# Two graph layers on one core: the output bias of the second stage as one product over stacked parts

## Chip, cores and metric

The kernel runs on one core of one Trainium2 chip. The metric is the device time of one execution in microseconds (us). The core has the engines TensorE (PE, with its weight loads PEld), VectorE (DVE), ScalarE (ACT), GpSimd (POOL) and SyncE (SP), and 16 DMA engines.

## What is computed

The reference works on 6250 nodes with 256 features and 100000 edges sorted by target. Four blocks follow one another, each added to its input after a layer norm: a graph layer, a soft mixture of 8 experts, a second graph layer, and a mixture that picks one of 32 experts. The change lies in the first mixture:

```python
w = softmax(feat @ Wr + br)                      # 8 gates per node
h = relu(bn(einsum('bfd,edh->bfeh', x, W1) + b1))
h = relu(bn(einsum('bfeh,ehk->bfek', h, W2) + b2))
y = einsum('bfeh,ehd->bfed', h, Wo) + bo         # bo: 8 x 256
out = einsum('bfed,fe->bfd', y, w)
```

So every node's row gets, beside the gated outputs of the experts, the sum over the 8 experts of gate times output bias: a product of the nodes' gates (nodes x 8) with `bo` (8 x 256). This document calls it the bias product.

## The kernel before, in words

The program is one `build` with three large parts between barriers: a preparation (layer norm, first projections, and a sort of the edges into lists), the second stage (the block that begins at line 1127: graph layer one, the 8-expert mixture, and the projection for graph layer two), and the third stage (from line 1806). There are 49 tiles of 128 nodes. The second stage takes them in 13 groups: the first has one tile, the other twelve have four (`WIDTHS`, line 48). Here "wide group" means one of the twelve.

The order is written out by hand in slots: every engine runs `for s in range(SLOTS)` and does in slot s what tables fixed at build time say. The tables are `READY` (line 1232, when a group's edges are summed), `FFN` (line 1233, when its experts begin), `AT` (line 1241, the steps of an expert), `DONE`, `NORM4`, `BASE`, and `USES` (line 1250), the list of the uses of PSUM bank 3. A wide group takes 16 slots, two for each expert.

In each of the first 196 slots (`EGROUPS`) 512 edges are handled. POOL gathers their source rows with four indirect DMAs into a ring of three buffers `got` (line 1324), and before it fills a buffer again it waits for the last reader (`s_mlo`, line 1322). ACT weighs the rows (`weigh`, line 1379) and rounds them to an upper part `mhi` (`upper_messages`, line 1388). DVE makes the one-hot matrix `hot` from `iota_f` (`one_hot`, line 1593) and the lower part `mlo` (`lower_messages`, line 1601). PE multiplies `hot` with both parts (`edges`, line 1483); it waits there for `s_mlo`.

The expert steps are products of float32r operands split into an upper and a lower part, three matmuls for one product (`three`, line 1312). `layer(0, n)` and `layer(1, n)` (line 1499) and `outputs(n)` (line 1520) are PE's. Between them ACT applies `relus` (line 1395: two activations at line 1409 and a rounding copy to `hhi` at line 1414), then DVE makes `hlo` (`lower_half`, line 1606), for which the next layer waits. `rl` is one buffer for both layers, so the next `relus` waits for `lower_half` of the one before it. DVE's `add_out` (line 1617) adds the gated outputs to the node rows.

Bank 3 is shared in turn by six kinds of use (`USES`): "turn" (transposes of the normalised rows), "logit", "gateT" (transposes of the gates), "bias", "turn4" and "prod". PE fills it in slot s (`make_bank`, line 1533) at the end of its slot, after it has waited on `s_free` for every earlier use to be read. ACT (`read_bank`, line 1416) or DVE reads it in slot s + 1. Each use adds one to `s_free`. For a group, "gateT" stands in slot READY + 7 and the bias products of its two pairs of tiles in READY + 8 and READY + 9. Before the change ACT copies the transposed gates to `gateT`, a float32 tile of 8 partitions (line 1427), PE multiplies 128 columns of it at a time with `bos` (8 x 256 float32, lines 1559 to 1561), and DVE's `output_bias` (line 1669) adds the result to the rows.

What one engine does within a slot stands in a fixed order. DVE's part, around the place that the change touches (lines 1692 to 1706):

```python
if s in AT[4]: add_out(AT[4][s], s)
if s - 1 in USE_AT and USES[USE_AT[s - 1]][1] == "bias": output_bias(...)
if s + 1 < EGROUPS: one_hot(s + 1)
if s in AT[2]: lower_half(1, AT[2][s])
if ... == "prod": lower_product(USE_AT[s - 1])
if s + 1 < EGROUPS: lower_messages(s + 1)
if s in AT[0]: lower_half(0, AT[0][s])
```

PE's slot is layer(0), edges, outputs, layer(1), make_bank. ACT's is relus(1), read_bank, weigh, relus(0), the rounding of the normalised rows, square roots, upper_messages, and in the first eight slots the rounding of the expert weights, three pieces a slot, whose lower parts DVE makes (line 1798). In the last group, whose edges are long done, the slots fall otherwise: "gateT" is read in a slot in which relus(1) and lower_half(1) stand too.

At line 1345 and behind it SP loads the small arrays, `bo` among them, and `s_small` counts them to 240; DVE waits for that count in slot 1 (line 1775).

## Time and profile before

| what | us |
| --- | --- |
| three runs | 3012.72, 3002.51, 3017.39 (median 3012.72) |
| profiled execution | 3008.19 |
| its span, first to last instruction | 3006.3 |
| PE busy over the span | 2719.2 (90%) |
| DVE busy | 2165.6 (72%) |
| POOL busy | 1939.8 (65%) |
| ACT busy | 1514.5 (50%) |

Shares are of the span. The profiled execution has 1.9 us outside its span. All times of single instructions below are of that one execution, counted from the start of its span. The second stage's gathers begin at about 413 us in it, its last bias product stands at 1745 us, and the third stage's first edge product at 1856.6 us.

### The profile page before, as it was taken

The page shows a single profiled execution, that of the slowest core. Times are in us where ns is not written, and L with a number is a line of the kernel's source. Part 1 is how long each engine was busy: PE and PEld are TensorE (multiplying, and loading weights), DVE is VectorE, ACT ScalarE, POOL GpSimd, SP SyncE. Part 2 cuts the span into 40 slices and gives each one's busy share as a digit, 9 for nine tenths or more (in the row PEclk, how much of TensorE's full clock was granted, in tenths as well). Part 3 has the DMA queues.
Part 4 walks back from the last instruction along what each step waited for, and adds up shares of the span by engine and source line. Part 5 has one row for each costly group of instructions (what it writes and reads, how often), then busy time and mean ns, then how long its engine had stood idle before and what let it go on. Part 6 is the DMA issues. An engine that isn't in the chain of part 4 may idle for free. (4 is left out here: it accounts for less than half of the span.)

```text
span 3006.3 us, 53462 instructions
## 1 busy us (share of the span) xinstructions
PE 2719.2 (90%) x18949; PEld 2484.4 (83%) x18949; DVE 2165.6 (72%) x5008; ACT 1514.5 (50%) x3146; POOL 1939.8 (65%) x1692
## 2 busy tenths in 40 slices
PE   5799935899999999999999993689999999999999
PEld 5789825788888888888888873689999999999998
DVE  8898836577777877877787655767777777777762
ACT  4377636788888888888888651111111111111111
POOL 0355557777777777777777204777777777777750
PEclk9999956899999999999999996789999999999999
DMA  2133454333333233333323105888888888788860
GB/s 73 6 80 77 91 141 143 92 97 94 96 108 110 79 111 111 97 94 109 107 81 108 46 22 159 210 209 201 215 215 207 208 206 211 195 204 208 203 153 15
DMA packets 241570, 390.22 MB, mean 130 GB/s; under 512 B 43258, under 2 KB 114834, under 8 KB 241042
## 3 DMA queue, kind: packets, MB, share of 16 engines
q0 software_dynamic: 163072, 310.24, 40.6%
q1 hardware_dynamic: 77940, 74.90, 7.9%
q8 instruction: 153, 2.51, 0.3%
q10 hardware_dynamic: 288, 1.61, 0.1%
q14 instruction: 117, 0.96, 0.1%
HBM read 343.43 MB, written 43.19 MB: 129 GB/s over the span
## 5 line engine op out<-in xcount | busy, mean ns | idle before, releaser
L1324 POOL DMA_INDIRECT f_got<-h_tab,list_cols x784 | 974.9, 1244 | 287.8 <-issue 220.2
L1994 POOL DMA_INDIRECT n_got<-h_tab,edge_cols x784 | 798.9, 1019 | 263.2 <-issue 232.3
L2046 ACT ACTIVATE n_hrh<-bank 128x512 fp32r<-128x512 f32 (+1 forms) x208 | 119.3, 574 | 924.5 <-PE bank L2116 924.5
L1609 DVE TENSOR_TENSOR f_hlo<-edge_cols,f_hhi 128x1024 fp32r<-128x1024 f32 (+1 forms) x208 | 241.8, 1162 | 300.0 <-ACT f_hhi L1414 299.4
L2095 PE MATMUL bank<-n_got,n_hot_h 128*128 128x256 f32 x1168 | 352.0, 301 | 70.1 <-DMA n_got<-h_tab,edge_cols 36.2
L1384 ACT ACTIVATE f_got<-f_got,list_cols 128x256 f32<-128x256 f32 x784 | 333.9, 497 | 150.2 <-DMA f_got<-h_tab,list_cols 150.1
L1495 PE MATMUL bank<-f_mhi,f_hot 128*128 128x256 f32 x1168 | 316.2, 304 | 80.8 <-DVE f_mlo L1603 80.8
L1409 ACT ACTIVATE edge_cols<-bank,f_shf,f_scl 128x512 f32<-128x512 f32 (+1 forms) x416 | 295.2, 744 | 118.5 <-PE bank L1315 84.8
L2096 PE MATMUL bank<-n_got,n_hot_h 128*128 128x256 f32 x1168 | 338.6, 290 | 0.0
L2097 PE MATMUL bank<-n_got,n_hot_l 128*128 128x256 f32 x1168 | 338.5, 290 | 0.0
L2197 DVE TENSOR_SCALAR n_hot_h<-list_cols,rel_f,edge_cols 128x256 fp32r<-128x256 f32 (+1 forms) x784 | 252.4, 389 | 117.2 <-PE bank L2097 117.1
L1495 PEld LDWEIGHTS bank<-f_mhi,f_hot 128*128 128x128 f32 x1168 | 236.4, 202 | 96.5 <-issue 91.9
L1496 PE MATMUL bank<-f_mlo,f_hot 128*128 128x256 f32 x1168 | 305.3, 295 | 0.0
L380 POOL DMA_INDIRECT list<-runs,off_i x98 | 156.0, 1592 | 224.7 <-DVE off_i L739 101.2
L2095 PEld LDWEIGHTS bank<-n_got,n_hot_h 128*128 128x128 f32 x1168 | 231.5, 198 | 82.5 <-DMA n_got<-h_tab,edge_cols 37.9
L2224 DVE SCALAR_TENSOR_TENSOR n_hrl<-bank,n_hrh 128x512 fp32r<-128x512 f32 (+1 forms) x208 | 135.9, 654 | 160.3 <-ACT n_hrh L2046 160.3
L1603 DVE TENSOR_TENSOR f_mlo<-f_got,f_mhi 128x1024 fp32r<-128x1024 f32 x196 | 238.9, 1219 | 17.1 <-ACT f_mhi L1393 17.1
L2197 DVE TENSOR_SCALAR n_hot_l<-list_cols,rel_f,edge_cols 128x256 fp32r<-128x256 f32 (+1 forms) x784 | 248.8, 396 | 0.0
L1496 PEld LDWEIGHTS bank<-f_mlo,f_hot 128*128 128x128 f32 x1168 | 237.0, 203 | 4.1
L2096 PEld LDWEIGHTS bank<-n_got,n_hot_h 128*128 128x128 f32 x1168 | 232.3, 199 | 1.7
L2097 PEld LDWEIGHTS bank<-n_got,n_hot_l 128*128 128x128 f32 x1168 | 232.0, 199 | 0.0
L1313 PE MATMUL bank<-f_whi,f_hhi 128*128 128x256 f32 x784 | 223.2, 285 | 5.6 <-DVE f_hlo L1609 5.6
(327 smaller groups left out, 7396.3 us busy)
## 6 DMA issues: line engine op xcount, KB each, us to landing
f_got<-h_tab,list_cols POOLq DMA_INDIRECT x784
n_got<-h_tab,edge_cols POOLq DMA_INDIRECT x784, 3.8
h_tab<-acc SPq DMA_DIRECT2D x37, 128.0 KB
edge_cols<-in_w SPq DMA_DIRECT2D x16, 256.0 KB, 3.2
xn<-acc_tab SPq DMA_DIRECT2D x8, 512.0 KB, 5.8
n_rows<-acc_tab SPq DMA_DIRECT2D x8, 512.0 KB, 5.6
out_rows<-n_rows SPq DMA_DIRECT2D x8, 512.0 KB, 4.6
acc<-in_x SPq DMA_DIRECT2D x4, 896.0 KB, 8.4
```

The source lines that it names most:

```text
L1324: nc.gpsimd.indirect_dma_start(got[:, s % RING0, u, :], None, h_tab[0], bass.IndirectOffsetOnAxis(gidx0[:, s * U + u:s * U + u + 1], 0), b ...
L1384: last = nc.scalar.activation(got[:, s % RING0, u, :], got[:, s % RING0, u, :], ACT.Copy, scale=w0_f[:, c:c + 1])
L1409: nc.scalar.activation(rl[:, m, 0:w], bank[(i + m) % 3][:, 0:w], ACT.Relu, bias=shf[:, l, e, m:m + 1], scale=scl[:, l, e, m:m + 1]).then_i ...
L1495: nc.tensor.matmul(tile_bank(t), lhs, mhi[:, s % 2, u, :], start=begins, stop=False)
L1496: last = nc.tensor.matmul(tile_bank(t), lhs, mlo[:, s % 2, u, :], start=False, stop=ends)
L1603: nc.vector.tensor_tensor(mlo[:, s % 2, :, :], got[:, s % RING0, :, :], mhi[:, s % 2, :, :].bitcast(F32), ALU.subtract).then_inc(s_mlo, 1)
L1609: nc.vector.tensor_tensor(hlo[l][:, :, 0:w], rl[:, :, 0:w], hhi[l][:, :, 0:w].bitcast(F32), ALU.subtract).then_inc(s_lo[l], 1)
L1994: nc.gpsimd.indirect_dma_start(got[:, s % RING, u, :], None, h_tab[1], bass.IndirectOffsetOnAxis(gidx[:, s * U + u:s * U + u + 1], 0), bou ...
L2095: nc.tensor.matmul(tile_bank(t), w_h, m_h, start=begins, stop=False)
L2096: nc.tensor.matmul(tile_bank(t), w_h, m_l, start=False, stop=False)
L2097: last = nc.tensor.matmul(tile_bank(t), w_l, m_h, start=False, stop=ends)
L2197: last = nc.vector.tensor_scalar(table[:, s % 2, u, 0:n], iota_f[:, 0:n], rel_n[:, c:c + 1], weight[:, c:c + 1], ALU.is_equal, ALU.mult)
```

## The change

It replaces the float32 bias product by one float32r product over more rows. `gateT` and `bos` become float32r tiles of 72 partitions (`STACK`). In `gateT`, partitions 0 to 7 and 64 to 71 hold the upper part of the gates, and partitions 32 to 39 the lower part. In `bos`, partitions 0 to 7 and 32 to 39 hold the upper part of the bias and 64 to 71 its lower part. All other partitions hold zeros. One matmul then sums upper times upper, lower times upper and upper times lower.

For each group ACT makes two copies of the transposed gates in place of one, counted by `s_ghi`, and DVE subtracts the upper part from bank 3 (`lower_gates`), which now frees the bank. `lower_gates` stands in DVE's slot behind `output_bias` and ahead of `one_hot`. Once, in slot 1, DVE writes zeros (three instructions) and ACT copies the bias twice; in slot 3 DVE makes the lower part. `iota_f` moves into the place of the old `bos` (row 6 of `xn`, now with all its partitions), and `bo` is loaded into a part of `xraw`.

```diff
@@ -1180,10 +1180,13 @@
             bnt = sb3("bnt", [P, 2, EXPERTS0, F])
             gws = sb3("gws", [P, F, EXPERTS0])
             gbs = sb3("gbs", [P, EXPERTS0])
-            bos = xn[0:EXPERTS0, 6, :]
+            HI_A, LO_A, HI_B, STACK = 0, 32, 64, 64 + EXPERTS0
+            bos = sb3("bos", [STACK, D], F32R)
+            s_bos = sem("f_bos")
+            s_ghi = sem("f_ghi")
             lws = sb3("lws", [P, F, D])
             lbs = sb3("lbs", [P, D])
-            iota_f = sb3("iota_f", [P, 2 * P])
+            iota_f = xn[:, 6, :]
             got = sb3("got", [P, RING0, U, D])
             mhi = sb3("mhi", [P, 2, U, D], F32R)
             mlo = sb3("mlo", [P, 2, U, D], F32R)
@@ -1197,13 +1200,14 @@
 
             xraw, rl = (edge_cols[:, b * F * W4:(b + 1) * F * W4].rearrange("p (f n) -> p f n", f=F) for b in range(2))
             iota_i = xraw[:, 0, 0:2 * P].bitcast(I32)
+            braw = xraw[0:EXPERTS0, 1, 0:D]
             xhi = sb3("xhi", [P, F, W4], F32R)
             xlo = sb3("xlo", [P, F, W4], F32R)
             x4 = sb3("x4", [P, F, 2 * P])
             glog = sb3("glog", [P, GS, EXPERTS0])
             gate = sb3("gate", [P, 2, GS, EXPERTS0])
             gm = sb3("gm", [P, GS])
-            gateT = sb3("gateT", [EXPERTS0, W4])
+            gateT = sb3("gateT", [STACK, W4], F32R)
             hhi = [sb3(f"hhi{l}", [P, F, W4], F32R) for l in range(2)]
             hlo = [sb3(f"hlo{l}", [P, F, W4], F32R) for l in range(2)]
 
@@ -1346,7 +1350,7 @@
                         sp.dma_start(bnp[:, l, a], arr).then_inc(s_small, 16)
                 sp.dma_start(gws[:, :, :], gw.rearrange("(f p) e -> p f e", p=P)).then_inc(s_small, 16)
                 sp.dma_start(gbs[:, :], gbr.partition_broadcast(P)).then_inc(s_small, 16)
-                sp.dma_start(bos[:, :], bo).then_inc(s_small, 16)
+                sp.dma_start(braw, bo).then_inc(s_small, 16)
                 sp.dma_start(lws[:, :, :], lw.rearrange("(f p) d -> p f d", p=P)).then_inc(s_small, 16)
                 sp.dma_start(lbs[:, :], lb.partition_broadcast(P)).then_inc(s_small, 16)
                 load(0)
@@ -1420,11 +1424,15 @@
                         act.wait_ge(s_made, i + 1)
                         if g:
                             act.wait_ge(s_xlo, g)
+                        else:
+                            act.wait_ge(s_bos, 6)
                         nc.scalar.activation(pair_of(xraw, j, w), turned(w), ACT.Copy).then_inc(s_free, 1)
                     elif what == "gateT":
                         act.wait_ge(s_made, i + 1)
                         n = width(g) * P
-                        nc.scalar.activation(gateT[:, 0:n], bank[3][0:EXPERTS0, 0:n], ACT.Copy).then_inc(s_free, 1)
+                        for at in (HI_A, HI_B):
+                            nc.scalar.activation(gateT[at:at + EXPERTS0, 0:n], bank[3][0:EXPERTS0, 0:n],
+                                                 ACT.Copy).then_inc(s_ghi, 1)
                     elif what == "turn4":
                         act.wait_ge(s_made, i + 1)
                         act.wait_ge(s_wlo, NPIECE)
@@ -1471,6 +1479,10 @@
                     if s + AHEAD < EGROUPS:
                         upper_messages(s + AHEAD)
                     if s == 1:
+                        act.wait_ge(s_small, 240)
+                        act.wait_ge(s_bos, 3)
+                        for at in (HI_A, LO_A):
+                            nc.scalar.activation(bos[at:at + EXPERTS0, :], braw, ACT.Copy).then_inc(s_bos, 1)
                         act.wait_ge(s_bn, 1)
                         nc.scalar.activation(scl[:, :, :, :], bnt[:, :, :, :], ACT.Sqrt).then_inc(s_bnroot, 1)
                     for i in range(s * PACE, min(s * PACE + PACE, NPIECE)):
@@ -1555,6 +1567,8 @@
                             last = nc.tensor.transpose(bank[3][0:EXPERTS0, k * P:(k + 1) * P], gate[:, g % 2, k, :],
                                                        ident[:, :])
                     elif what == "bias":
+                        if g == 0:
+                            pe.wait_ge(s_bos, 6)
                         for k in range(w):
                             last = nc.tensor.matmul(bank[3][:, k * D:(k + 1) * D],
                                                     gateT[:, (2 * j + k) * P:(2 * j + k + 1) * P], bos[:, :],
@@ -1677,6 +1691,15 @@
                     nc.vector.tensor_tensor(rows2, bank[3][:, 0:w * D].rearrange("p (k d) -> p k d", d=D), rows2,
                                             ALU.add).then_inc(s_free, 1)
 
+                def lower_gates(i):
+
+                    _, _, g, _ = USES[i]
+                    n = width(g) * P
+                    dve.wait_ge(s_ghi, 2 * g + 2)
+                    nc.vector.tensor_tensor(gateT[LO_A:LO_A + EXPERTS0, 0:n], bank[3][0:EXPERTS0, 0:n],
+                                            gateT[HI_A:HI_A + EXPERTS0, 0:n].bitcast(F32),
+                                            ALU.subtract).then_inc(s_free, 1)
+
                 def lower_product(i):
 
                     _, _, g, j = USES[i]
@@ -1694,6 +1717,8 @@
                         add_out(AT[4][s], s)
                     if s - 1 in USE_AT and USES[USE_AT[s - 1]][1] == "bias":
                         output_bias(USE_AT[s - 1], s)
+                    if s - 1 in USE_AT and USES[USE_AT[s - 1]][1] == "gateT":
+                        lower_gates(USE_AT[s - 1])
                     if s + 1 < EGROUPS:
                         one_hot(s + 1)
                     if s in AT[2]:
@@ -1774,7 +1799,12 @@
                     if s == 1:
                         dve.wait_ge(s_small, 240)
                         nc.vector.tensor_scalar(bnt[:, :, :, :], bnp[:, :, 4], BN_EPS, None, ALU.add).then_inc(s_bn, 1)
+                        for blank in (bos[:, :], gateT[:, 0:D], gateT[:, D:2 * D]):
+                            nc.vector.tensor_scalar(blank, iota_f[0:STACK, :], 0.0, None, ALU.mult).then_inc(s_bos, 1)
                     if s == 3:
+                        dve.wait_ge(s_bos, 5)
+                        nc.vector.tensor_tensor(bos[HI_B:HI_B + EXPERTS0, :], braw,
+                                                bos[HI_A:HI_A + EXPERTS0, :].bitcast(F32), ALU.subtract).then_inc(s_bos, 1)
                         dve.wait_ge(s_bnroot, 1)
                         nc.vector.reciprocal(scl[:, :, :, :], scl[:, :, :, :]).then_inc(s_bn, 1)
                         dve.wait_ge(s_bn, 2)
```

## Rows read from the trace of the kernel before

**Rows 1.** The profile's page, first part: busy us (share of span) and instructions.

```profile
PE 2719.2 (90%) x18949; PEld 2484.4 (83%) x18949; DVE 2165.6 (72%) x5008; ACT 1514.5 (50%) x3146; POOL 1939.8 (65%) x1692
```

**Rows 2.** Stretches: length, then busy of PE, PEld, DVE, ACT, POOL; PE clock, DMA share, GB/s.

```profile
600.00:700.00 100.00, 96.76 (x610) 86.15 (x610) 76.06 (x126) 87.27 (x139) 76.73 (x65) 1.00 0.32 95
...
1500.00:1600.00 100.00, 97.41 (x620) 87.33 (x620) 78.92 (x135) 85.87 (x136) 76.17 (x62) 1.00 0.34 102
```

**Rows 3.** What PE waited for, 600 to 1600 us: total us, times, longest.

```profile
PE bank L1495 <- DVE f_mlo L1603: 24.4, 30, 2.0
PE bank L1313 <- DVE f_hlo L1609: 8.2, 6, 2.1
```

**Rows 4.** The bias product's line: PE durations in ns (min/median/max), first and last start.

```profile
L1559 PE MATMUL bank<-xn,f_gateT x98: 374/374/478, 512.5 to 1744.9; 8*128 8x256 f32 x98
```

**Rows 5.** Timeline of PE at both bias products of one group: start, us, then idle before.

```profile
1025.01 1.13 PE L1559 MATMUL bank<-xn,f_gateT 8*128 8x256 f32 x4
1026.06 0.50 PE L1313 MATMUL bank<-f_xhi,f_whi 128*128 128x512 f32 x1
...
1030.02 1.13 PE L1559 MATMUL bank<-xn,f_gateT 8*128 8x256 f32 x4
1031.33 0.36 PE L1495 MATMUL bank<-f_mhi,f_hot 128*128 128x256 f32 x1 [0.19 <-DVE f_mlo L1603]
1031.53 0.28 PE L1496 MATMUL bank<-f_mlo,f_hot 128*128 128x256 f32 x1
1031.65 0.28 PE L1495 MATMUL bank<-f_mhi,f_hot 128*128 128x256 f32 x1
```

**Rows 6.** Timeline of DVE over the same place.

```profile
1019.32 1.23 DVE L1609 TENSOR_TENSOR f_hlo<-edge_cols,f_hhi 128x1024 fp32r<-128x1024 f32 x1 [1.66 <-ACT f_hhi L1414]
...
1022.38 0.68 DVE L1597 TENSOR_TENSOR f_hot<-f_iota_f,rel_f 128x512 fp32r<-128x512 f32 x1
...
1027.09 0.69 DVE L1677 TENSOR_TENSOR xn<-bank,xn 128x512 f32<-128x512 f32 x1
1027.70 1.22 DVE L1597 TENSOR_TENSOR f_hot<-f_iota_f,rel_f 128x1024 fp32r<-128x1024 f32 x1
...
1029.96 1.22 DVE L1603 TENSOR_TENSOR f_mlo<-f_got,f_mhi 128x1024 fp32r<-128x1024 f32 x1
...
1038.15 1.21 DVE L1603 TENSOR_TENSOR f_mlo<-f_got,f_mhi 128x1024 fp32r<-128x1024 f32 x1
```

**Rows 7.** Timeline of ACT over the same place.

```profile
1020.14 0.57 ACT L1427 ACTIVATE f_gateT<-bank 8x512 f32<-8x512 f32 x1
1021.76 1.71 ACT L1384 ACTIVATE f_got<-f_got,list_cols 128x256 f32<-128x256 f32 x4 [1.05 <-DMA f_got<-h_tab,list_cols]
...
1027.30 1.06 ACT L1414 ACTIVATE f_hhi<-edge_cols 128x1024 fp32r<-128x1024 f32 x1
```

**Rows 8.** Timeline of POOL behind it: the gathers.

```profile
1030.10 1.97 POOL L1324 DMA_INDIRECT f_got<-h_tab,list_cols  x1 [0.30 <-issue]
...
1040.21 1.01 POOL L1324 DMA_INDIRECT f_got<-h_tab,list_cols  x1 [2.81 <-DVE f_mlo L1603]
```

**Rows 9.** Timeline of PE: first edge product behind the second bias product, two more groups.

```profile
614.18 0.37 PE L1495 MATMUL bank<-f_mhi,f_hot 128*128 128x256 f32 x1
...
1659.20 0.36 PE L1495 MATMUL bank<-f_mhi,f_hot 128*128 128x256 f32 x1 [0.20 <-DVE f_mlo L1603]
```

**Rows 10.** Timelines of ACT, DVE and PE in the last group.

```profile
1735.90 0.57 ACT L1427 ACTIVATE f_gateT<-bank 8x512 f32<-8x512 f32 x1
1736.03 1.23 DVE L1609 TENSOR_TENSOR f_hlo<-edge_cols,f_hhi 128x1024 fp32r<-128x1024 f32 x1 [2.43 <-ACT f_hhi L1414]
...
1739.86 1.23 DVE L1609 TENSOR_TENSOR f_hlo<-edge_cols,f_hhi 128x1024 fp32r<-128x1024 f32 x1 [2.61 <-ACT f_hhi L1414]
...
1741.29 0.40 PE L1313 MATMUL bank<-f_hhi,f_whi 128*128 128x512 f32 x1
```

**Rows 11.** Timeline of DVE in slot 1, at the stage's start.

```profile
441.87 1.29 DVE L1798 TENSOR_TENSOR f_wlo<-edge_cols,f_whi 128x512 fp32r<-128x512 f32 x2 [2.92 <-ACT f_whi L1479]
```

## Prediction, made before the changed kernel was run

> **What bounds the kernel now.** I looked first at how busy the engines are, over the whole span and then by stretches of the second stage, because the change touches only that stage. The page has PE at 90% and DVE at 72% of the span [rows 1]. From 600 to 1600 us, where the wide groups run with edges beside them, the stretches have PE at 97 of 100 us, at a granted clock of 1.00 (the upper level, 2.4 GHz), ACT at 85 to 87, DVE at 76 to 79 and POOL at 76 [rows 2]. The reader is to see in this a stage that looks bound by PE, so that time taken off PE should come straight off the total.
>
> The waits say where that holds and where it does not. Over those 1000 us PE waited 24.4 us in 30 places for the lower messages of DVE before an edge product, and 8.2 us in 6 places for a lower half of DVE [rows 3]: nearly ten groups, so three to four short waits a group. PE is late for nobody at those places; it catches up with DVE. So the question is whether one of the three waits stands right behind the bias products. I read the timelines of PE, DVE, ACT and POOL around them, in the group whose first bias product starts at 1025.01.
>
> It does. PE finishes the second bias product and then waits 0.19 us for `mlo` before the edge product at 1031.33 [rows 5]. That `mlo` is the last link of a chain on DVE: it begins with a lower half at 1019.32 that waited 1.66 us for ACT, and ends at 1029.96 + 1.22 = 1031.18. Between them stand 13 more rows of the timeline without one wait before them [rows 6]. The same wait of 0.19 to 0.67 us for `mlo` stands behind the second bias product in ten of the eleven wide groups that still have edges (the last of them at 1659.20); in the first, at 614.18, there is none, and DVE is done only 0.1 us earlier [rows 9]. So PE and DVE arrive there together. A microsecond less on PE is a microsecond more of waiting; a microsecond more on DVE is a microsecond later.
>
> **The change, part by part.** *The product itself.* The 49 float32 products have 98 PE records [rows 4], two each. Two products occupy PE from 1025.01 to 1026.06, 1.05 us; single-pass products of 256 columns follow one another at 0.12 us (1031.53 to 1031.65) [rows 5], so two take 0.24. That frees 0.81 us for two tiles, 1.6 us for a wide group, 49 x 0.405 = 20 us in all. That the new operand has 72 rows in place of 8 I cost at nothing: the edge products at that pace have 128. The Trainium skill, "FP8 and Floating Point Precision", section "TensorE Precision Notes", has true float32 as four passes through the array; four passes at the pace of the row would be 0.48 us a tile, and the trace's 0.52 agrees. What of these 20 us shortens the stage? In the eleven groups with edges PE would reach the edge product of 1031.33 some 1.6 us earlier and wait for the same `mlo`. The first product's saving lets layer 0 of the next expert start earlier, but its `relus` waits for DVE's lower half at 1028.83, which is in the chain. I take nothing, and keep 20 us as the bound on the gain.
>
> *The new subtraction on DVE.* `lower_gates` stands ahead of `one_hot` in that very chain, before the row at 1022.38. Its nearest row is `output_bias`, also 512 elements a partition with one operand in PSUM: 0.69 us long, and 1027.70 - 1027.09 = 0.61 until the next one starts [rows 6]. I take 0.61; eight partitions in place of 128 I don't count as a gain, since ACT's copy of only 8 partitions takes 0.57 us too [rows 7]. The bounds are 0.3 (half the row, if few partitions help after all) and 0.69. It lies wholly on the path: 11 x 0.61 = 6.7 us. Whoever waits behind it waits too: `one_hot`, `mlo`, the lower half that frees `relus` of the next expert, and the `mlo` at 1038.15, for which POOL's gather at 1040.21 waits 2.81 us [rows 8]. So POOL is moved with the chain; no engine passes this place on another path.
>
> *The second copy on ACT.* It adds 0.57 us for each of the 12 wide groups. In the group read ACT's next work waited 1.05 us for a gather [rows 7], which covers it; other groups have no such wait. Where it isn't covered, the rounding to `hhi` at 1027.30 ends 0.57 later than 1028.36, at 1028.93. DVE's lower half, which needs it, starts at 1028.83 now and 0.61 later after the change, so DVE's own delay covers ACT's. And does `lower_gates` wait for the copy? It would end at 1020.14 + 2 x 0.57 = 1021.3, and DVE gets there at 1022.38: no, with 1.1 us to spare. If that cover went, each group would pay up to 0.57.
>
> *The last wide group.* There lower_half(1) stands in the same slot. The gates' copy starts at 1735.90 and the lower half at 1736.03 [rows 10]. With `lower_gates` ahead of it, that half waits for both copies and the subtraction: 1735.90 + 1.14 + 0.05 + 0.61 = 1737.7, later by 1.7. The next `relus`, its lower half (1739.86 to 1741.09) and PE's layer at 1741.29 follow it link by link, with nothing between them, so I take 1.6 us. PE's saving of 1.6 us lies beside that chain. Bounds: 0 (if the saving on PE replaces it) and 1.7.
>
> *The start.* Three blanks on DVE and two bias copies on ACT in slot 1, one small subtraction in slot 3. DVE idles 2.92 us behind the blanks [rows 11], but for ACT, which now waits for the blanks (which have no row; 0.3 us each for 256 elements, an estimate from half of the 512-element row) and makes two copies of 256 elements at 0.3. ACT waits for gathers before most of its weighings there, and DVE's chain isn't reached before POOL's: I take 0, bounds 0 to 1.5. The first group has one tile and runs beside the same gathers: 0. The load of `bo` goes to another address, in its old place in SP's queue; `iota_f` is read as before: 0.
>
> **The sum** is 6.7 + 1.6 = 8.3 us slower. Against the profiled execution it makes 3008.2 + 8.3 = 3016.5. The median of the runs is 4.5 us above the profiled one and the runs spread over 15 us, so for a median I take 3012.7 + 8.3 = 3021.0. About 0.5% (15 us) is what a measurement of this kernel can tell from no change, so this forecast counts as no change, on the slow side.
>
> **Rivals.** *PE is the bound and the gain arrives.* For it: PE is at 97%. Against it: ten waits for `mlo` exactly there. It needs DVE's chain to be elastic, for instance if its start, a wait for ACT at 1019.32, moved up with PE. Full: 3012.7 - 20 = 2993; half, if the other waits of a group (1 to 2 us each) take the rest: 3003.
>
> *DVE's chain and ACT's copy add up.* Place: the read of "gateT" in DVE's slot. It decides once ACT's second copy ends later than DVE's arrival, or if POOL's late gathers no longer cover it. Price: 11 x (0.61 + 0.57) + 1.7 = 14.7, with 1.5 at the start 16: 3029.
>
> *The delay is absorbed.* If the waits behind (1 to 2 us, at the second half of the group) are set by POOL's gathers and not by the chain, they shrink by 0.61 each. Against it: the gather at 1040.21 itself waits for the chain. Then only the last group remains: 3014.
>
> *The gathers stretch.* One takes 1.97 us in place of 1.01 beside DVE's work [rows 8]; one more of these a group is 11 x 0.96 = 10.6 if it is not covered. The wait of 2.81 us at 1040.21 covers it, so this would show as 3021 still; uncovered, 3031. The Trainium skill, "SBUF — State Buffer", section "SBUF: two separate sides", has GpSimd blocked by a VectorE operation with two SBUF inputs, or in a two-port mode, and so its descriptors late. By that rule `lower_gates`, with one input in PSUM, stretches none.
>
> *It doesn't do what it says:* the new product is no faster; then PE is late by nothing, and the time is the forecast's.
>
> **How the numbers follow.** Forecast 0.55; absorbed 0.13; added up 0.14; stretched 0.05; gain in full or half 0.13. Forecast and neighbours give 3014 to 3029, the spread of medians some 5 us more. The range runs from 3005 to 3031, which leaves out the gain in full and part of the last cases. Faster than 2998 takes the full gain: 0.09. Slower than 3028 takes the upper cases, or the forecast with a high median: 0.21. The rest, 0.70, is no change.
>
> **What would show it.** The product's line should have 49 PE records in place of 98, and two should take 0.24 us. `lower_gates` should show 0.6 to 0.7 us in 12 of 13. The wait for `mlo` behind the second bias product should grow from 0.2 to 2.4 us (1.6 + 0.6), PE's busy time fall by some 20 us and its waits grow by 28. From one group's first bias product to the next (105 us) 0.6 more should stand. In the last group the lower half should start some 1.7 us later against the gates' copy. I am wrong if that wait stays under 1 us, or if the groups come closer together.

## The result, and the profile after

The changed kernel takes 3034.49 us, the kernel before 3012.93 in the same set of runs (six each, taken in turn): ratio 1.0074, 95% interval 1.0052 to 1.0097. So it is slower by 22 us. The forecast had the right sign and the right place, but with 8.3 us too small a size; 3034.49 lies outside the range of 3005 to 3031. Two more sets of runs of the same kernel gave 1.0067 and 1.0061 (experiments below): 18 to 22 us in all three.

The page of the changed kernel, engines' busy time:

```profile
span 3032.3 us, 53399 instructions
PE 2717.2 (90%) x18900; PEld 2490.8 (82%) x18900; DVE 2181.6 (72%) x5025; ACT 1523.6 (50%) x3161; POOL 1907.0 (63%) x1692
```

PE has its 49 records less, yet its busy time is only 2 us below the 2719.2 of [rows 1]; the clock explains most of that, further down. DVE has 16 us more. The groups of instructions of the new lines, the product and the subtraction (busy us, mean ns of one, idle before):

```profile
L1573 PE MATMUL bank<-f_bos,f_gateT 72*128 72x256 f32 x49 | 10.8, 301 | 1.0 <-DVE f_gateT L1699 0.5 <-DVE xn L1691 0.2
```

```profile
L1699 DVE TENSOR_TENSOR f_gateT<-bank,f_gateT 8x512 fp32r<-8x512 f32 (+1 forms) x13 | 8.4, 649 | 6.4 <-ACT f_gateT L1434 6.0
```

The waits of PE over the same 1000 us as [rows 3] (line waited at, releaser, us in total, times, longest):

```profile
PE bank L1507 <- DVE f_mlo L1617: 52.1, 32, 3.0
PE bank L1317 <- DVE f_xlo L1736: 1.5, 2, 0.8
PE bank L1317 <- DVE f_hlo L1623: 1.5, 2, 1.1
```

The wait for `mlo` has doubled, from 24.4 us in 30 places to 52.1 in 32. Where, the timeline of PE in one group shows, at both bias products:

```profile
1250.39 0.40 PE L1573 MATMUL bank<-f_bos,f_gateT 72*128 72x256 f32 x2
1250.63 0.39 PE L1317 MATMUL bank<-f_xhi,f_whi 128*128 128x512 f32 x1
...
1254.41 0.50 PE L1573 MATMUL bank<-f_bos,f_gateT 72*128 72x256 f32 x2
1257.92 0.36 PE L1507 MATMUL bank<-f_mhi,f_hot 128*128 128x256 f32 x1 [3.01 <-DVE f_mlo L1617]
```

Two tiles' products take 1250.63 - 1250.39 = 0.24 us, against 1.05 in [rows 5]: the product does what the change says. And all that it gives back ends in the wait behind the second one, 0.2 us before and 3.01 now; over the eleven wide groups with edges these waits sum to 2.8 us before and 32.0 after. DVE over the same place:

```profile
1244.79 1.23 DVE L1623 TENSOR_TENSOR f_hlo<-edge_cols,f_hhi 128x1024 fp32r<-128x1024 f32 x1 [1.66 <-ACT f_hhi L1418]
1245.93 1.40 DVE L1775 BATCH_NORM_STATS2 f_stats<-acc 128x6 f32<-128x256 f32 x4
1247.37 0.38 DVE L1779 BATCH_NORM_AGGREGATE f_mean<-f_stats 128x2 f32<-128x6 f32 x4
1247.78 0.42 DVE L1782 TENSOR_SCALAR f_var<-f_mean 128x4 f32<-128x4 f32 x1
1248.23 0.68 DVE L1699 TENSOR_TENSOR f_gateT<-bank,f_gateT 8x512 fp32r<-8x512 f32 x1
1248.94 0.69 DVE L1611 TENSOR_TENSOR f_hot<-xn,rel_f 128x512 fp32r<-128x512 f32 x1
1249.55 1.22 DVE L1617 TENSOR_TENSOR f_mlo<-f_got,f_mhi 128x1024 fp32r<-128x1024 f32 x1
...
1256.56 1.21 DVE L1617 TENSOR_TENSOR f_mlo<-f_got,f_mhi 128x1024 fp32r<-128x1024 f32 x1
```

The chain of [rows 6], from the lower half that waits 1.66 us to the end of the second `mlo`, runs from 1244.79 to 1256.56 + 1.21 = 1257.77: 13.0 us here, 11.9 there (1019.32 to 1031.18). Over the eleven wide groups with edges its mean is 12.88 us after (11.56 in the first, 13.31 in one, 12.96 to 12.99 in the others) and 11.77 before (10.68 in the first, 11.88 in the others). The price of `lower_gates` in this chain is thus 1.11 us a group, where 0.61 were predicted. Its own length is as predicted (0.68). What wasn't predicted stands in the gaps: `lower_gates` starts 1248.23 - 1247.78 = 0.45 after `f_var`, and `one_hot` 1248.94 - 1248.23 = 0.71 after `lower_gates`. In the kernel before, `one_hot` starts 0.08 us after `f_var`, which lasts 0.41, so the two run into each other; timeline of DVE in the kernel before, inside the stretch of [rows 6]:

```profile
1021.89 0.38 DVE L1754 BATCH_NORM_AGGREGATE f_mean<-f_stats 128x2 f32<-128x6 f32 x4
1022.30 0.41 DVE L1757 TENSOR_SCALAR f_var<-f_mean 128x4 f32<-128x4 f32 x1
```

(the next row is the 1022.38 of [rows 6]). So 0.08 us became 0.45 + 0.71 = 1.16, in ten of the eleven groups, to 0.02. In the first wide group `f_var` is shorter (0.15 us) and `lower_gates` starts 0.22 behind it.

The pitch of the groups grew by more than the chain. From one wide group's first bias product to the next it is 104.5 us before, as the mean of ten intervals (608.10 to 1652.87), and 106.5 after (610.15 to 1675.62): 2.1 more, where 0.6 was forecast and the chain gives 1.11. In two more profiles of the changed kernel it is 106.0 and 106.5.

The last wide group went as forecast. ACT, then DVE, then PE in it, and at the end the accumulation on DVE from which its chain is counted, after and before:

```profile
1762.89 1.18 ACT L1434 ACTIVATE f_gateT<-bank 8x512 fp32r<-8x512 f32 x2
```

```profile
1764.10 0.68 DVE L1699 TENSOR_TENSOR f_gateT<-bank,f_gateT 8x512 fp32r<-8x512 f32 x1 [3.52 <-ACT f_gateT L1434]
1764.81 1.22 DVE L1623 TENSOR_TENSOR f_hlo<-edge_cols,f_hhi 128x1024 fp32r<-128x1024 f32 x1
...
1768.64 1.23 DVE L1623 TENSOR_TENSOR f_hlo<-edge_cols,f_hhi 128x1024 fp32r<-128x1024 f32 x1 [2.61 <-ACT f_hhi L1418]
```

```profile
1769.92 0.50 PE L1317 MATMUL bank<-f_hhi,f_whi 128*128 128x512 f32 x1 [0.69 <-DVE f_hlo L1623]
```

```profile
1758.92 1.66 DVE L1640 SCALAR_TENSOR_TENSOR xn<-bank,f_gate,xn 128x256 f32<-128x256 f32 x4
```

```profile
1731.94 1.66 DVE L1626 SCALAR_TENSOR_TENSOR xn<-bank,f_gate,xn 128x256 f32<-128x256 f32 x4
```

The lower half starts 1764.81 - 1762.89 = 1.92 us after the gates' copy, 0.13 in [rows 10], so 1.8 later; from the start of the last accumulation on DVE to the layer on PE it is 1769.92 - 1758.92 = 11.0 us in place of 1741.29 - 1731.94 = 9.35, 1.65 more (1.6 to 1.7 predicted).

One thing the forecast did not have. PE's granted clock behind the long wait, in windows of the changed kernel (columns: us, then busy us and instructions of PE, weight loads, DVE, ACT, POOL, then the clock):

```profile
1259.00:1263.00 4.00, 4.00 (x23) 4.00 (x23) 3.58 (x10) 3.82 (x7) 3.09 (x4) 0.57 0.24 70
1366.00:1372.00 6.00, 5.97 (x28) 6.00 (x29) 4.48 (x12) 4.88 (x8) 4.36 (x4) 0.51 0.24 68
```

and the same place in the kernel before (behind the 1031.33 of [rows 5]):

```profile
1031.40:1035.40 4.00, 4.00 (x34) 4.00 (x35) 2.57 (x8) 3.59 (x7) 3.09 (x4) 1.00 0.22 66
```

After a wait of 2 to 3 us PE runs for some 3 to 6 us near the lower of its two levels (0.5 is 1.2 GHz, 1.00 is 2.4 GHz): 23 matmuls in 4 us, not 34. This happens behind nine of these eleven waits, some 39 us at half pace in all, and behind none before (39: from the granted clock of the 6 us behind each wait). Half of that, some 20 us, is busy time that full pace wouldn't have, and it about cancels the 16.9 us that the bias product's records lost (27.7 us before, 10.8 after): hence PE's nearly unchanged total. It made a second theory: is it the clock, rather than the chain, that makes the change slow?

### The profile page after: what moved, and what is told of

The parts are those of the page before. It is cut to its first block and busy times, and to the rows that moved or that the text cites. A ratio compares the mean times of both kernels' runs of the same rounds, so it can differ in the third digit from the quotient of the medians.

```text
span 3032.3 us, 53399 instructions
## 1 busy us (share of the span) xinstructions
PE 2717.2 (90%) x18900; PEld 2490.8 (82%) x18900; DVE 2181.6 (72%) x5025; ACT 1523.6 (50%) x3161; POOL 1907.0 (63%) x1692
## 5 line engine op out<-in xcount | busy, mean ns | idle before, releaser
L1328 POOL DMA_INDIRECT f_got<-h_tab,list_cols x784 | 943.3, 1203 | 342.6 <-issue 218.2
L1507 PE MATMUL bank<-f_mhi,f_hot 128*128 128x256 f32 x1168 | 326.9, 311 | 115.1 <-DVE f_mlo L1617 114.9
L1507 PEld LDWEIGHTS bank<-f_mhi,f_hot 128*128 128x128 f32 x1168 | 244.6, 209 | 129.8 <-issue 125.0
L1508 PE MATMUL bank<-f_mlo,f_hot 128*128 128x256 f32 x1168 | 316.1, 302 | 0.0
L1508 PEld LDWEIGHTS bank<-f_mlo,f_hot 128*128 128x128 f32 x1168 | 245.6, 210 | 4.1
```

What stands on the lines that cost most here:

```text
L1328: nc.gpsimd.indirect_dma_start(got[:, s % RING0, u, :], None, h_tab[0], bass.IndirectOffsetOnAxis(gidx0[:, s * U + u:s * U + u + 1], 0), b ...
L1507: nc.tensor.matmul(tile_bank(t), lhs, mhi[:, s % 2, u, :], start=begins, stop=False)
L1508: last = nc.tensor.matmul(tile_bank(t), lhs, mlo[:, s % 2, u, :], start=False, stop=ends)
```

## The experiments

The theories: the clock that falls behind the long wait costs the time (theory A in the expectations); or the cost lies in DVE's subtraction, longer on the chain than predicted; or in ACT's second copy; or in the work at the stage's start. Theories B and C in the expectations put all of it on the added work of DVE and ACT; D puts it on the subtraction, E on ACT's copy as well. Each run was measured beside the kernel before on the same chip. The chips differ: the kernel before takes 3012 to 3014 us on two of them, 3185 on one and 3233 to 3237 on two more, the difference mostly in the third stage. So each time is given as a ratio to the kernel before on its chip; by 3013 us, 0.001 is 3 us. Several of these kernels leave out a part of the product, as their expectations say; the rest is issued as in the changed kernel.

**The clock, first try: each bias product four times.**

```
-    last = matmul(bank[3]..., gateT..., bos...)
+    for again in range(4):
+        last = matmul(bank[3]..., gateT..., bos...)
```

> The changed kernel, with each tile's bias product issued four times into the same place, so that PE is occupied about as long as by the float32 product. ACT and DVE do what they do in the changed kernel. In its trace PE waits 3.0 us for the lower messages behind the second bias product, and in nine of eleven wide groups its matmuls then run at half pace for 3 to 5 us. Theory A (the time freed on PE becomes a wait, and the wait lowers PE's granted clock): no stretch at half pace behind the bias products, that wait at about 1.0 us, and 13 to 17 us back from the change's 21.6: 8 us slower than before (4 to 12). Theory B (DVE's subtraction and ACT's second copy cost all of it, the clock is beside the path): as slow as the changed kernel, 18 to 24 us slower than before.

Measured: 1.0037 (1.0013 to 1.0062), 12 us, on the chip of 3233 us. The wait shrank to 1.7 to 2.3 us in ten of the eleven groups (0.24 in the first), where theory A had expected 1.0, and five groups still show the half pace. The time lies at the upper end of theory A's 4 to 12 us and below theory B's 18 to 24. Inconclusive; a fuller filling was needed.

**Without the subtraction and the second copy**, single-pass product kept.

```
-    for at in (HI_A, HI_B): activation(gateT[at:at+8], bank[3]...)
+    activation(gateT[HI_A:HI_A+8], bank[3]...)
...
-    if ...== "gateT": lower_gates(...)
```

> The changed kernel without lower_gates and without ACT's second copy: the lower part of the gates and the product with the bias's lower part are left out. PE's product is as short as in the changed kernel, and DVE and ACT do per group what they did before the change. Theory A: PE reaches the edge product 1.6 us early and waits 1.8 to 2.0 us there; some of the stretches at half pace stay, so 2 to 12 us slower than before. Rival (PE's 20 us arrive once nothing is added to DVE): 10 to 20 us faster. Theory B: 0 to 3 us slower (the work at the stage's start alone).

Measured: 1.0007 (0.9987 to 1.0028), same chip. The wait for `mlo` was 2.5 us in nine of the eleven groups and the half pace stood behind six of them, and still the time was that of the kernel before, within its interval of -4 to +9 us. So neither the long wait nor the lower clock behind it costs the 22 us, though a smaller cost fits the interval; and of the 20 us saved on PE none arrives that can be seen.

**The subtraction and the copy with the float32 product.**

```
-    matmul(..., gateT[:, ...], bos[:, :])
+    matmul(..., gateT[0:8, ...].bitcast(F32), bos[0:8, :].bitcast(F32))
```

> The changed kernel with the float32 product over 8 rows in its old place (of the bias, the upper part; the lower parts are made but not used). So ACT and DVE have all the added work and PE's product is as long as before. Theory A: no stretch at half pace behind the bias products; 0.6 us for each of eleven groups, 1.7 in the last, 1 to 2 at the start: 10 us slower than before (6 to 13). Theory B: 18 to 24 us slower, as the changed kernel.

Measured: 1.0040 (1.0020 to 1.0061), 13 us, same chip: slower without the new product. So a cost lies in the work that makes its operand. Its size does not decide between the theories: 13 us is the upper end of theory A's 6 to 13 and below theory B's 18 to 24, the changed kernel itself was not run on this chip, and against theory A's words PE still waited 1.3 to 2.1 us in nine groups, with the half pace behind six.

**The start alone**, all else as before.

> The float32 product over 8 rows, one copy of the gates by ACT and no lower_gates: of the change only the work at the stage's start is left (three blanks and one subtraction on DVE, two copies on ACT), the moved tiles, and the first wait. Theory A: 1 to 2 us slower than before, lower messages 1 to 2 us later from slot 2 on. Rival (the start is covered by the gathers): 0. Theory B: 0 to 2.

Measured: 1.0011 (0.9990 to 1.0032), and once more on another chip (below) 1.0014 (0.9993 to 1.0035).

**The changed kernel again, and each product eight times**, on the chip of 3012 us.

> The changed kernel itself, to stand beside the others on one chip; the first four variants ran on a chip whose kernel before takes 3233 us in place of 3013. There the float32 product with all the added work of ACT and DVE was 0.40% slower than before, with the fourfold product 0.37%, with only the work at the start 0.11%. Theory A (half of the loss is PE's clock): 0.6 to 0.9% slower, stretches at half pace behind the second bias product in most wide groups. Theory C (on such a chip the added work on DVE is all of it): 0.3 to 0.5%, as the fourfold product.

> The changed kernel with each tile's bias product issued eight times into the same place: PE is occupied for 1.9 us a pair and so nearly until the lower messages come. Theory A: PE's wait behind the second bias product under 0.5 us, no half pace there, and 5 to 15 us faster than the changed kernel on this chip. Theory C: the same time as the changed kernel within 4 us. Rival (PE is the bound after all): 10 to 20 us slower than the changed kernel, for 49 x 7 more products of 0.12 us are 41 us of PE.

Measured: 1.0067 (1.0050 to 1.0084) for the changed kernel, which lies in theory A's range and above theory C's, and 1.0057 (1.0039 to 1.0076) with eight products. Those fill the wait: PE's timeline and, behind it, the clock in the run with eight:

```profile
1250.58 2.07 PE L1574 MATMUL bank<-f_bos,f_gateT 72*128 72x256 f32 x16
1252.90 0.36 PE L1507 MATMUL bank<-f_mhi,f_hot 128*128 128x256 f32 x1 [0.25 <-DVE f_mlo L1618]
```

```profile
1254.20:1258.20 4.00, 4.00 (x34) 3.92 (x33) 3.80 (x11) 3.60 (x6) 3.08 (x4) 1.00 0.23 66
```

The wait is 0.25 us, the clock 1.00, no group at half pace behind the bias products, and the time is the same within both intervals: the means are 2 us apart, give or take 4, where theory A wanted 5 to 15. Theory A falls as the cause; up to some 6 us for the clock are not excluded by this pair. The repeats also lengthen PE's work at a group's first product, so the run shows the sum of both; DVE's chain is 12.88 us in it as in the changed kernel. It fits that the half pace lies in time that the groups have to spare elsewhere.

**The gates split before they are transposed.** DVE makes [upper, upper, lower] parts of the small gate tile (32 numbers a partition) in the slot before, PE transposes 24 columns, ACT copies once, `lower_gates` is gone; the product stays single-pass, over 24 rows. And the same with each product five times.

```
+    for at in (HI_A, HI_B): tensor_copy(gcat[:, 0:w, at:at+8], gate[...])
+    tensor_tensor(gcat[:, 0:w, LO_A:LO_A+8], gate[...], gcat[... HI_A ...], subtract)
...
-    transpose(bank[3][0:8, ...], gate[...])
+    transpose(bank[3][0:24, ...], gcat[...])
...
-    if ...== "gateT": lower_gates(...)
```

> The gates are split before they are transposed: DVE makes upper, upper and lower part of 128 x 32 gates in its slot of the softmax (three instructions of some 0.2 us, where it waits for ACT soon after), PE transposes 24 columns, and ACT makes one copy of 24 x 512. The product is single-pass over 24 rows, with no blanks. lower_gates and the second copy are gone. If DVE's subtraction in the chain is the cost: 8 to 14 us faster than the changed kernel, and about as the kernel before (within 5 us). Theory A adds that PE's wait behind the bias products is 1.8 to 2.5 us, with stretches at half pace in about half the groups, so 0 to 6 us slower than before.

> As the one before, with each product issued five times, so that PE is occupied as long as by the float32 product. Theory A: no half pace behind the bias products, 2 to 8 us faster than without the repeats, and within 3 us of the kernel before. Theory C: no difference from the kernel without the repeats.

Measured: 1.0007 (0.9993 to 1.0022) and 1.0019 (1.0006 to 1.0031), on the same chip of 3012 us as the two runs above. The chain is 11.77 us again, and with it 17 of the 21 us are gone (medians: changed 3033.06, this one 3016.35, before 3011.94; 8 to 14 were expected), though PE is 1.6 us a group faster than before and waits 1.5 to 1.9 us at `mlo` in ten of the eleven groups. The kernel differs from the changed one in more than the chain: one copy on ACT in place of two, no blanks, and no `lower_gates` in the last group. Filling the wait gained nothing here either: 2.5 us slower by the medians, where theory A wanted 2 to 8 faster.

**The subtraction and the copy apart.** Four kernels on one chip of 3237 us: the subtraction without the second copy; the copies without the subtraction; the start alone again; and the subtraction with its output on partitions 0 to 7 in place of 32 to 39.

```
-    tensor_tensor(gateT[LO_A:LO_A+8, 0:n], bank[3][0:8...], gateT[HI_A...], subtract)
+    tensor_tensor(gateT[HI_A:HI_A+8, 0:n], bank[3][0:8...], gateT[HI_A...], subtract)
```

> The changed kernel without ACT's second copy (the product with the bias's lower part is left out); lower_gates stays. The repeats showed no half pace behind the bias products and the same time as the changed kernel, so the theory of the clock is dropped, and what stands is: lower_gates takes 1.08 us of DVE's chain (from the start of the row before it to the start of one_hot it is 1.15 in place of 0.08), not 0.61. Theory D (DVE's subtraction is nearly all of the per-group cost): 11 x 1.08 + 1.1 in the last group + 2 to 4 at the start = 15 to 17 us slower than before, 1 to 3 faster than the changed kernel. Theory E (ACT's copy costs its 0.57 us in each group on top): 12 to 14 slower than before, 7 faster than the changed kernel.

> The changed kernel without lower_gates (the lower part of the gates is left out); ACT makes both copies and the second frees the bank. Theory D: 2 to 5 us slower than before (the start, and at most 1 us for the copy in the last group). Theory E: 8 to 11 us slower.

> The work at the stage's start alone, with the float32 product over 8 rows, as in an earlier variant, whose 0.11% on a slower chip had an interval from -0.10 to 0.32. Both theories: 1 to 4 us slower than before. If it is 0, the 4 us of the kernel that splits the gates first come from its own three instructions or from PE's shorter product.

> The changed kernel, but lower_gates writes to the partitions 0 to 7 that it reads, over the upper part, in place of 32 to 39 (so the product of upper gates with upper bias is left out). If the 0.37 us that the row before lower_gates takes longer, and the missing overlap behind it, come from writing to other partitions than are read: the row before takes 0.08 again, lower_gates 0.61, and the kernel is 11 x 0.45 = 5 us faster than the changed one. If they come from the wait or from reading PSUM: no difference.

Measured, in that order: 1.0045 (1.0023 to 1.0067), 1.0015 (0.9993 to 1.0037), 1.0014 (0.9993 to 1.0035), 1.0017 (0.9992 to 1.0041). The copy is worth 0.0001 on top of the start: nothing that can be measured, as predicted. The subtraction is worth 0.0031, 10 us, with intervals of 0.002 either way on each ratio; the two kernels differ in the new product too, which brought nothing above. With its output on partitions 0 to 7 most of that is gone; this kernel writes over the upper part of the gates, so its product leaves out upper times upper. DVE's timeline in that run:

```profile
833.18 0.41 DVE L1782 TENSOR_SCALAR f_var<-f_mean 128x4 f32<-128x4 f32 x1
833.26 0.67 DVE L1699 TENSOR_TENSOR f_gateT<-bank,f_gateT 8x512 fp32r<-8x512 f32 x1
833.86 0.67 DVE L1611 TENSOR_TENSOR f_hot<-xn,rel_f 128x512 fp32r<-128x512 f32 x1
```

The gaps are 0.08 and 0.60, and the chain is 12.40 us, +0.63 over 11.77: the predicted price. But this run also wrote in place. The next batch, on the chip of 3185 us, tells place from partition, and doubles the link.

**Another tile on partitions 0 to 7, and the subtraction twice.**

```
-    tensor_tensor(gateT[LO_A:LO_A+8, 0:n], bank[3]..., gateT[HI_A...], subtract)
+    tensor_tensor(x4[0:8, ...], bank[3]..., gateT[HI_A...], subtract)
```

```
+    tensor_tensor(x4[LO_A:LO_A+8, ...], bank[3]..., gateT[HI_A...], subtract)
     tensor_tensor(gateT[LO_A:LO_A+8, 0:n], bank[3]..., gateT[HI_A...], subtract)
```

> The changed kernel with its subtraction writing partitions 0 to 7 of another tile (x4) in place of partitions 32 to 39 of gateT; the lower part of the gates stays at zero in the bias product, everything else is issued as in the change. In the run that wrote in place over partitions 0 to 7, the subtraction started 0.08 us after the one before it and the next instruction followed 0.60 later (chain +0.61 us a group); in the changed kernel these are 0.44 and 0.71 (chain +1.11). If the extra 0.5 us comes from writing other partitions than the ones read, this run shows 0.08 and 0.60 as well, a chain of 12.40 us, and some 5 us less than the changed kernel: +14 to +16 us against the kernel before. If it comes from writing another tile than the operand, the chain stays at 12.88 us and the time at +20 us (ratio 1.007).

> The changed kernel with its subtraction issued twice in a row: the added one writes partitions 32 to 39 of another tile (x4), whose values nothing reads. If the time of the change is the length of the vector engine's chain, a second link of the same kind costs the same again: the chain of a wide group goes from 12.88 to 13.6 to 14.0 us (0.7 if the two follow each other at 0.71, 1.1 if at the full price), eleven groups make 8 to 12 us and the last wide group another 0.7 to 1.1, so 9 to 13 us above the changed kernel, +29 to +34 us against the kernel before (ratio 1.010 to 1.011). If the chain only uses up a slack that is now gone for another reason, or the chain is hidden, it stays at the changed kernel's +20 us (1.007).

Measured: 1.0018 (0.9999 to 1.0037) and 1.0055 (1.0033 to 1.0076). DVE's timelines of the two:

```profile
1036.63 0.41 DVE L1782 TENSOR_SCALAR f_var<-f_mean 128x4 f32<-128x4 f32 x1
1036.71 0.67 DVE L1699 TENSOR_TENSOR f_x<-bank,f_gateT 8x512 fp32r<-8x512 f32 x1
1037.31 0.67 DVE L1611 TENSOR_TENSOR f_hot<-xn,rel_f 128x512 fp32r<-128x512 f32 x1
```

```profile
1043.38 0.41 DVE L1786 TENSOR_SCALAR f_var<-f_mean 128x4 f32<-128x4 f32 x1
1043.82 0.68 DVE L1699 TENSOR_TENSOR f_x<-bank,f_gateT 8x512 fp32r<-8x512 f32 x1
1044.43 0.67 DVE L1703 TENSOR_TENSOR f_gateT<-bank,f_gateT 8x512 fp32r<-8x512 f32 x1
1045.13 0.69 DVE L1611 TENSOR_TENSOR f_hot<-xn,rel_f 128x512 fp32r<-128x512 f32 x1
```

Another tile on the same partitions costs no more than in place (0.08, 0.60; chain 12.40). It is the partitions; the wait for ACT's copy and the read of PSUM are the same in all of these kernels. The times are less sharp than the gaps, and the expectation missed: this run was to lie 14 to 16 us above the kernel before and lies 6 us above (0 to 12). The run in place, with the same chain, came out at 1.0017. Both times are lower than this chain gives, so the 0.63 us a group is shown by the traces and not by the times. And of two subtractions that both write from partition 32, only the first starts late (0.44) and only what follows the second does (0.70); between them it is 0.61. The price is paid where the output moves from partition 0 to 32 and again where it moves back, 0.37 and 0.11 us, not by each instruction. The Trainium skill, "VectorE: DVE Perf Modes", section "Two Vector instructions with no wait between them", has just this: an instruction whose output starts in another group of 32 partitions than the last output into that memory is held until every earlier one has finished. By that rule `lower_gates` and `one_hot` are held in the changed kernel, none is in the run on partitions 0 to 7, and of the doubled pair only the first, with `one_hot`; the trace agrees in each of these gaps, and the 0.45 and 0.71 are the lengths of the instructions waited for (0.42 and 0.68) plus 0.03.

The time follows the chain in the doubled run too: its chain is 13.46 us, 1.06 more than 12.40, and 11 x 1.06 = 11.7 us; measured between the two medians 3201.63 - 3194.37 = 7.3, by the ratios 0.0037 x 3185 = 11.8. The expectation for the doubled run, made from the chip of 3013 us (29 to 34 us), was too high: 17.5.

**The kernel before once more, and a shorter chain.** The second of these is the kernel with the gates split first, with `output_bias` of a group's first two tiles issued behind `mlo`, where DVE idles, and the second bias product issued by PE behind the next slot's edges.

```
+    if s - 1 in USE_AT and second_bias(USE_AT[s - 1]):
+        make_bank(USE_AT[s - 1])
...
-    if s in USE_AT:
+    if s in USE_AT and not second_bias(USE_AT[s]):
...
-    if s - 1 in USE_AT and USES[USE_AT[s - 1]][1] == "bias":
+    if s - 1 in USE_AT and second_bias(USE_AT[s - 1]):
         output_bias(USE_AT[s - 1], s)
...
+    if s - 1 in USE_AT and USES[USE_AT[s - 1]][1] == "bias" and not second_bias(USE_AT[s - 1]):
+        output_bias(USE_AT[s - 1], s)
```

> The kernel before, unchanged, as a second profile and as a measure of how far two sets of the same kernel differ. Ratio 1.000 within 0.0015. The ten wide groups of its first profile took 1045.2 us, those of the two kernels that split the gates before transposing them 1049.2 and 1050.8, at the same chain. If this profile shows 1045 again, 4 us of the change lie outside the chain; if it shows 1048 to 1051, the first profile was a good one and the chain is the whole cost.

> The kernel that splits the gates before transposing them (1.0007 against before), with the first output bias of a group taken out of the vector engine's chain: it is issued behind the lower messages, where that engine idles, and the second bias product is issued by the tensor engine behind the next slot's edges. The chain goes from 11.77 to 11.2 us. If the chain sets the pace of a group, eleven groups give 6 to 7 us: 5 us under the kernel before (ratio 0.998, 0.997 to 1.000). If the chain is only one of several things that arrive together there, the time stays at 1.0007. If the moved product delays the edges of its new slot, it is slower than 1.0007.

Measured: 1.0001 (0.9984 to 1.0019) for the kernel before against itself, and 0.9976 (0.9961 to 0.9991) for the shorter chain, 3179.39 us against 3184.52. That one beats the kernel before, on whose chip the changed kernel was not run. Its chain is 11.05 us, and where the kernel before has `output_bias` between the accumulations and `one_hot`, it has nothing:

```profile
1032.67 1.66 DVE L1644 SCALAR_TENSOR_TENSOR xn<-bank,f_gate,xn 128x256 f32<-128x256 f32 x4
1034.25 1.22 DVE L1615 TENSOR_TENSOR f_hot<-xn,rel_f 128x1024 fp32r<-128x1024 f32 x1
1035.38 1.25 DVE L1627 TENSOR_TENSOR f_hlo<-edge_cols,f_hhi 128x1024 fp32r<-128x1024 f32 x1
1036.56 1.21 DVE L1621 TENSOR_TENSOR f_mlo<-f_got,f_mhi 128x1024 fp32r<-128x1024 f32 x1
1037.69 0.68 DVE L1702 TENSOR_TENSOR xn<-bank,xn 128x512 f32<-128x512 f32 x1
```

On the question of the stage's remaining 4 us the kernel before says little: from the first wide group's first bias product to the eleventh's it took 1061.0 us in this profile and 1044.8 in the first, on different chips, so single profiles of different chips don't resolve it.

**The same reordering with the float32 product, and the changed kernel on that chip** (kernel before 3013.71 us).

> The changed kernel once more, beside the next run and on its chip. Measured so far: 1.0074 and 1.0067 on a chip where the kernel before takes 3013 us. The slower chips have not run it itself: there its copy without the second ACT copy gave 1.0045, and a chain of 13.46 us (against 12.88 here) gave 1.0055. If the cost of the chain is the same on every chip it comes out at 1.005 to 1.007; if the chips differ in it, a slower chip shows 1.003 to 1.005.

> The kernel before, float32 product and all, with only the reordering of the run that beat it: the first output bias behind the lower messages, the second bias product behind the next slot's edges. The chain of the vector engine is 0.61 us shorter. If the chain alone sets the pace and the product's form is worth nothing, it gives the same 0.9976 (0.996 to 0.999) with float32 products. If the single-pass product starts to pay once the wait behind it is gone, this run lies 10 to 20 us above that one: 1.000 to 1.004, since the tensor engine's 1.6 us a group are then no longer covered by a wait.

Measured: 1.0061 (1.0046 to 1.0075) for the changed kernel; 0.9998 (0.9989 to 1.0007) for the reordering with float32. Its chain is 11.09 us, as short as the one that won, and it gains nothing that shows, where the chain would give 11 x 0.68 = 7.5. Set side by side: PE 1.6 us shorter alone 1.0007, DVE's chain 0.7 shorter alone 0.9998, both 0.9976. That fits two engines that arrive together, where taking time from one shows nothing until the other gives too. It is not shown, for two reasons. The third ratio comes from another chip than the second, and the two kernels were not run on one. And the reordering has a cost of its own: from the last group's first bias product (1737.31) to the third stage's first edge product (1860.68) it is 123.4 us here and 119.3 in the kernel before, 4.1 more, with a wait of 1.92 on PE and its clock at 0.50 for the 6 us behind it. The ten group intervals are 2.3 us shorter together (1042.45 against 1044.77), where the chain would give 6.8.

## Why the prediction was wrong

*What bounds the stage:* right, as far as the change goes. PE at 97% looked like the bound, the wait behind the second bias product said that DVE arrives with it, and PE's saving went into that wait (the row at 1257.92, and 1.0007 both for the run without subtraction and copy and for the gates split first).

*The product itself:* right: 49 records, 0.24 us for two, 0.405 saved a tile, none of it seen in the time.

*The subtraction on DVE:* the step that failed. The place, the chain and the count of eleven were right; the term was 0.61 us a group and measured 1.11, 12.2 us in place of 6.7. That is 5.5 of the 13.5 us between the forecast of 3021.0 and the measured 3034.49; with this term right the forecast would have been 3026.5, so the rest of the miss has other owners (below). I took the pitch of `output_bias`, a neighbour that reads and writes the same partitions as the instructions around it, and priced `lower_gates` as one more of its kind. It writes partitions 32 to 39 between two that write from 0, and the row that would have told me to doubt was in the trace: `one_hot` starts 0.08 us behind an `f_var` of 0.41, an overlap that a new neighbour can break. My upper bound of 0.69 was its own length, which is no bound on what it does to the instruction behind it. With the output on partitions 0 to 7 the prediction's 0.61 comes out in the chain (0.63).

*The second copy on ACT:* right at nothing (1.0015 against 1.0014), hidden where the forecast said, with the two waits of DVE for the gates' copies (6.0 us in the group's line) in the first group, of one tile, and the last.

*The last wide group:* right, 1.65 us.

*The start:* taken as 0, bound 1.5. Alone it measured 1.0011 and 1.0014, some 4 us, but each interval holds 1. The trace has a bit of it: DVE's wait for ACT in slot 1 is 4.05 us against 2.92 in [rows 11], and the fourth `mlo` came 1.7 us later after the first gather in the first profile, yet not in two others of the same kernel. Not settled.

*The sum:* 12.2 + 1.65 + 0 to 4 makes 14 to 18 us, measured 18 to 22. Some 4 us have no owner. The profiles place them in the intervals between the groups: the ten together are 15.5, 20.0 and 20.7 us longer in three profiles of the changed kernel, all beside one profile of the kernel before, where the chain gives 11. What lengthens them beyond the chain stays open; profiles of the changed kernel differ by 5 us among themselves.

*The signs:* the wait was to grow to 2.4 us and grew to 3.0, the missing 0.5 being the same 0.5. The groups were to stand 0.6 us further apart and stand 1.6 to 2.1 further apart, a sign that failed in size and that the 1.11 of the chain does not fill. The wait did not stay under 1 us, nor did the groups come closer together, so the conditions for being wrong in kind didn't arise. "PE's busy time falls by 20" failed (it fell by 2), for the lower clock refilled it; busy time was a poor sign, the wait a good one.

*The rivals:* the two that add up (3029) had the size nearly right for a wrong reason: ACT's copy was its 0.57, and the copy costs nothing. Full or half gain: fell. Absorbed: fell. Stretched gathers: fell, as POOL's busy time is 33 us less (1907.0 against 1939.8 in [rows 1]), not more.

## What to carry over

When an instruction is put into a chain on the vector engine, look at the start-to-start gaps around the place, not only at its own length: neighbours that overlap (0.08 us behind an instruction of 0.41) lose the overlap if the new one writes from another 32-partition start, and the same data laid out so that outputs stay at one start (or made earlier, on a smaller tile, as in the run at 1.0007) costs half or nothing in the chain. When two engines arrive together at a wait, price a change on each alone at zero gain and at full loss; the runs here fit that a gain needs both, so try the two in one kernel.

## What the runs showed of the hardware

- A vector instruction that wrote from partition 32, between others that wrote from 0, started 0.44 us behind its predecessor in place of 0.08, and the next started 0.71 behind it in place of 0.60; two of them in a row were 0.61 apart.
- Eight partitions cost DVE what 128 cost: 0.68 us for 512 elements a partition against 0.69 for `one_hot`.
- After waits of 2 to 3 us PE's granted clock stood at 0.51 to 0.57 over stretches of 4 to 6 us (matmuls 0.21 us apart in place of 0.12). Removing every such stretch changed the time from 1.0067 to 1.0057, within the intervals (2 us, give or take 4).
- Five chips ran the kernel before in 3012 to 3237 us, with intervals of one ratio of 0.001 to 0.002; ratios carry over between chips better than microseconds, but not exactly (the changed kernel 1.006 to 1.007 on chips of 3013 us; without its second copy, 1.0045 on one of 3237).
